# A fused transformer-style block on one core: four steps of the delta branch stand one slot later in a hand-written schedule

## The reference, cut to what matters

```python
x = x + 0.5 * ffn(layernorm(x))          # first pass through the experts
x = x + mamba(layernorm(x))              # selective scan block
x = x + 0.5 * ffn(layernorm(x))          # second pass, same weights

def mamba(x):                            # x: 32 sequences x 256 tokens x 128 channels
    x_in, z = split(x @ W_in + b_in)     # 256 inner channels each
    x_conv = silu(causal_conv4(x_in) + conv_b)
    Bm, Cm = split(x_conv @ W_xp + b_xp)             # 16 states each
    delta = softplus(x_conv @ W_dt + b_dt)           # the "step size", 256 channels
    h[t] = exp(delta * A) * h[t-1] + delta * x_conv * Bm[t]      # for each of 16 states
    y = sum over states of h * Cm + D_skip * x_conv
    out = (y * silu(z)) @ W_out + b_out
    return alpha * (x + out - mean) / (std + eps) + beta

def ffn(x):                              # 8 experts of width 176, top 2, plus a shared one of width 352
    w = softmax weights of the two largest of x @ Wg
    return sum_e w[e] * ((silu(x @ W1[e]) * (x @ W2[e])) @ W3[e]) + (silu(x @ Ws1) * (x @ Ws2)) @ Ws3
```

## Time and profile before

| what | value |
| --- | --- |
| median of the runs | 1838.47 us (1837.09 to 1841.13) |
| profiled execution, own time | 1839.04 us |
| its span, first to last instruction | 1837.3 us |
| mean granted TensorE clock | 0.959 of full |
| ACT table loads at the decays, the silus, `in0`/`in1`, `sp_ln` | 124, 111, 30, 16, of 1283 ns each |

### The profile page before, as it was taken

One profiled execution on the slowest core, in us unless ns is written; L12 is line 12 of the kernel. 1 busy time (PEld: TensorE's weight loads), 2 busy tenths in 40 slices (PEclk: granted clock), 3 DMA queues, 4 the chain that ended last, 5 costly groups with the idle time before them and its releaser, 6 DMA issues.

```text
span 1837.3 us, 24041 instructions
## 1 busy us (share of the span) xinstructions
PE 1658.7 (90%) x7378; PEld 1001.5 (55%) x7378; DVE 1478.3 (80%) x2241; ACT 1266.2 (69%) x2030; POOL 1445.7 (79%) x1366
## 2 busy tenths in 40 slices
PE   5898788999999999999999999999999999958488
PEld 3454445556555555656555555656555555534255
DVE  1438889989798988989798988989898998989732
ACT  2367678787877778776867777786877777665422
POOL 3336869888898988888888888888898888887753
PEclk9998889999999999999999999999999999969599
DMA  6026768687776868686777867777677868767642
GB/s 158 24 87 141 180 150 193 160 205 173 185 184 162 207 156 201 158 194 170 178 184 170 201 158 189 181 187 184 168 190 172 196 156 192 184 152 186 143 104 69
DMA packets 121287, 304.54 MB, mean 166 GB/s; under 512 B 19299, under 2 KB 40518, under 8 KB 106822
## 3 DMA queue, kind: packets, MB, share of 16 engines
q0 software_dynamic: 18432, 125.84, 34.4%
q1 hardware_dynamic: 98406, 174.46, 33.3%
q10 hardware_dynamic: 4320, 2.71, 0.5%
HBM read 167.67 MB, written 5.24 MB: 94 GB/s over the span
## 4 chain that ended last, share of the span: by engine, by line
POOL 43%; DMA 23%; issue 14%; PE 9%; DVE 7%; ACT 1%; SPq 1%; POOLq 0%; ACTq 0%; DVEq 0%
DMA yacc<-prod 19%; POOL prod L623 18%; POOL gated L555 14%; DVE hist L924 4%; DMA crow<-c_rows 3%; POOL yacc L619 2%; PE ps_y L1090 2%; DVE ps_db L876 2%; POOL yacc L640 1%; PE ps_h1a L1076 1%; SPq L418 1%; PE ps_h2a L1098 1%; PE ps_h1b L1076 1%; PE ps_h2b L1098 1%; POOL xres L610 1%
## 5 line engine op out<-in xcount | busy, mean ns | idle before, releaser
L623 POOL TENSOR_TENSOR prod<-hist,crow 128x1024 f32<-128x1024 f32 x224 | 556.5, 2484 | 204.7 <-DVE hist L924 171.0
L1090 PEld LDWEIGHTS ps_y<-down_w,gated 128*128 128x128 f32 (+1 forms) x3584 | 474.0, 196 | 276.4 <-issue 160.1
L924 DVE TENSOR_TENSOR_SCAN hist<-decay,ps_db 128x1024 f32<-128x1024 f32 x256 | 583.3, 2278 | 2.8
L555 POOL TENSOR_TENSOR gated<-gated,silu 128x512 f32<-128x512 f32 x352 | 493.3, 1450 | 74.4 <-DVE gated L904 71.4
L1090 PE MATMUL ps_y<-down_w,gated 128*128 128x128 f32 (+1 forms) x3584 | 491.8, 282 | 58.0 <-POOL gated L555 56.3
L876 DVE TENSOR_TENSOR ps_db<-du,ps_db 128x1024 f32<-128x1024 f32 x256 | 313.2, 1224 | 114.2 <-PE ps_db L1058 112.1
L686 ACT ACTIVATE decay<-delta,a_neg 128x510 f32<-128x510 f32 x512 | 326.8, 709 | 3.7 <-DVE delta L965 2.2
L706 ACT ACTIVATE silu<-ps_h1a 128x512 f32<-128x512 f32 (+1 forms) x224 | 132.9, 593 | 194.8 <-PE ps_h1a L1076 194.6
L1076 PE MATMUL ps_h1b<-xnT,up_w 128*128 128x512 f32 x448 | 236.7, 610 | 3.6 <-ACT silu L706 3.1
L1098 PE MATMUL ps_h2a<-xnT,up_w 128*128 128x512 f32 (+1 forms) x448 | 236.1, 609 | 1.9 <-DVE gated L904 1.9
L1076 PE MATMUL ps_h1a<-xnT,up_w 128*128 128x512 f32 (+1 forms) x448 | 236.4, 609 | 0.0
(11 more groups left out here) (136 smaller groups left out, 1937.5 us busy)
## 6 DMA issues: line engine op xcount, KB each, us to landing
yacc<-prod POOLq DMA_DIRECT2D x112, 1024.0 KB, 10.0
crow<-c_rows SPq DMA_DIRECT2D x128, 512.0 KB, 5.0
wrow<-w_rows SPq DMA_DIRECT2D x320, 128.0 KB, 6.3
wrow<-w_rows SPq DMA_DIRECT2D x64, 224.0 KB, 7.0
wrow<-w_rows SPq DMA_DIRECT2D x64, 192.0 KB, 6.4
wrow<-w_rows SPq DMA_DIRECT2D x64, 160.0 KB, 2.9
yacc<-yacc POOLq DMA_DIRECT2D x16, 512.0 KB, 7.8
wrow<-w_rows SPq DMA_DIRECT2D x64, 96.0 KB, 2.9
```

The costliest lines, as they stand in the source:

```text
L555: nc.gpsimd.tensor_tensor(gated[:, pos % NGATE, :], gated[:, pos % NGATE, :], silu[:, (pos + NCHUNK * f_parity(of, f)) % NSILU, :], ALU.mu ...
L623: nc.gpsimd.tensor_tensor(prod[:, (pair - 1 + odd) % 2, s % 2, :, :], hist[:, s % 2, :, :], c_all, ALU.mult).then_inc(prod_done, 1)
L924: nc.vector.tensor_tensor_scan(hist[:, s % 2, :, :].rearrange("p h t -> p (h t)"), decay[:, s % NA, :, :, :].rearrange("p h b t -> p (h b ...
L1090: ins = nc.tensor.matmul(ps_y[:, t * C:(t + 1) * C], gated[0:rd, posd % NGATE, t * P:(t + 1) * P], down_w[0:rd, jd, :], start=(posd == 0 a ...
```

## The change

`dt1` goes from slot 18 to slot 19, `sp_exp` and `xproj` from slot 20 to 21, `sp_ln` from slot 22 to 23. `dt0`, `bparts`, `bsplit` and `delta` stay. In slot 19 `dt1` stands ahead of `stats1`, in slot 23 `sp_ln` stands ahead of `xT1`. `sp_exp` still comes last in its slot on ACT, behind the decays, but slot 21 has none. `START_PLAN` follows `PLAN`.

The rest of the diff puts the helpers that count semaphore values in another form: the functions that could take k as a register value lose that case, and the counts (`turn`, `ffn_no`, `route_no`, `stats_no`, the norms' chain) are looked up in lists that are made from the plan once. The plans are reached through dictionaries, and each step may name another iteration than the slot's own; no entry does so. The order of all other steps and what each waits for stay the same.

```diff
-        15: ["in3", "ln_scale"], 16: ["wT0", "ln_shift"], 17: ["dt0"], 18: ["dt1", "ln_add"], 19: ["stats1"],
-        20: ["sp_exp", "xproj", "scale1"], 21: ["addy1"], 22: ["norm1", "sp_ln", "bparts"], 23: ["xT1", "bsplit"], 24: ["logits1"],
+        15: ["in3", "ln_scale"], 16: ["wT0", "ln_shift"], 17: ["dt0"], 18: ["ln_add"], 19: ["dt1", "stats1"],
+        20: ["scale1"], 21: ["addy1", "sp_exp", "xproj"], 22: ["norm1", "bparts"], 23: ["sp_ln", "xT1", "bsplit"], 24: ["logits1"],
...
+    ALL = [(name, it) for k in range(-2, G + 2) for slot in range(SLOTS) for name, it in steps(k, slot)]
+    MISC = {step: n + 1 for n, step in enumerate(s for s in ALL if s[0] in MISC_NAMES)}
...
+    def turn(it, name):
+
+        return MISC[(name, it)]
...
-                    if "sp_exp" in plan(k).get(slot, []) and lead(k):
-
-                        act.wait_ge(softplus_chain, (HALVES + 1) * (k + 2) - 1)
-                        nc.scalar.activation(dtmp[:], dtmp[:], ACT.Exp, scale=-1.0).then_inc(softplus_chain, 1)
-
-            iterations(act, body)
+                    for step, it in steps(k, slot):
+                        if step == "sp_exp":
+
+                            act.wait_ge(softplus_chain, (HALVES + 1) * (it + 2) - 1)
+                            nc.scalar.activation(dtmp[:], dtmp[:], ACT.Exp, scale=-1.0).then_inc(softplus_chain, 1)
```

More of the change, by code:

```diff
@@ L91, in macaron_kernel @@
     }
[L93 to L100, removed]
     SETUP_MADE, SETUP_TAPS, SETUP_EDGE = 16, 24, 28
-    def first(k):
-        return isinstance(k, int) and k == -2
+    PLANS = {k: START_PLAN for k in range(-2, FULL)}
+    UNITS = {k: START_UNIT for k in range(-2, FULL)}
+    SP_PLANS = {k: START_SP for k in range(-2, FULL)}
     def enters(k):
-        return not isinstance(k, int) or 0 <= k + 2 < G
+        return 0 <= k + 2 < G
@@ L126, in before @@
[L126 to L187, removed]
+        return 0 <= k - 2 < G
@@ new lines, in macaron_kernel @@
+    ROLES = [(enters, ["stats0", "scale0", "norm0", "xT0", "logits0", "rcopy0", "route0", "tilt0", "weights0", "wT0"]),
+             (lead, ["addy0", "stats2", "scale2", "norm2", "xT2", "in0a", "in0", "in1a", "in1", "in2", "in3", "dt0", "dt1",
+                     "sp_exp", "sp_ln", "xproj", "bparts", "bsplit", "cT", "bT", "delta", "du"]),
+             (tail, ["fold", "gate_y0", "gate_y1", "outproj", "resid", "stats3", "scale3", "ln_norm", "ln_scale",
+                     "ln_shift", "ln_add", "stats1", "scale1", "norm1", "xT1", "logits1", "rcopy1", "route1", "tilt1",
+                     "weights1", "wT1"]),
+             (last, ["addy1"])]
@@ L189, in iterations, with w_turn, unit, home @@
+    def w_turn(it, f, e):
+        n = ECHUNK * ffn_no(it, f) + e
+        return n % NW, 2 * 16 * (n // NW + 1)
+    def unit(k, slot, lag):
+        return UNIT_AT.get((k + 2) * SLOTS + slot - lag)
+    def home(group):
+        return group % XS
+    def iterations(body):
         for k in range(-2, G + 2):
@@ L422, in body @@
                 for slot in range(SLOTS):
[L423 to L445, removed]
@@ L707, in body @@
+                        nc.scalar.activation(silu[0:r, (pos + NCHUNK * f_parity(of, f)) % NSILU, :],
                                              ps_h1[pos % 2][0:r, :], ACT.Silu).then_inc(silu_done, 1)
-                    for step in plan(k).get(slot, []):
-                        if step == "xT0" and enters(k) or step == "xT1" and tail(k) or step == "xT2" and lead(k):
-                            take(k, step)
+                    for step, it in steps(k, slot):
+                        nxt, entering, ahead, behind = 1 - it % 2, home(it + 2), home(it + 1), home(it - 1)
+                        if step == "xT0" or step == "xT1" or step == "xT2":
+                            take(it, step)
@@ L1166, in body @@
                             ins.then_inc(misc_full, 1)
-                    if slot == SETUP_EDGE and first(k):
+                    if slot == SETUP_EDGE and k == -2:
                         make_edge()
```

448 lines of the change are left out of this document (246 added, 202 removed).

## The result

The changed kernel takes **1854.42 us** (median of 4 runs, 1853.21 to 1862.09), the kernel before beside it 1839.8 (1837.09 to 1841.81). The ratio is 1.0089 (95% interval 1.0072 to 1.0107), some 15 to 16 us. The profiled execution is the slowest of the four, 1862.09 with a span of 1860.4; the other three are 1853.21, 1853.84 and 1855.0.

What follows compares the result with a forecast made beforehand. It took PE, 96% busy, as the bound, with `row_b(24)` setting short iterations; twelve times 2.67 us (32.0) less 9.9 swallowed by long iterations gave +22.1 us: 1861.1 for the profiled execution, median 1860, range 1842 to 1872.

Steps and rivals of the forecast that it cites:

- Part 1: `dt1` to slot 19: its 1.03 us wait goes, PE waits 2.0 us for POOL instead, `row_b(20)` 0.9 us later.
- Part 2: `xproj` to slot 21: the same work stands ahead of `row_b(22)` in either order, so nothing from there on.
- Part 3: `sp_exp` to slot 21: two more table loads, transposes of `norm1`'s tile wait 1.8 us, `row_b(24)` 2.67 us later in all.
- whatever delays `row_b(24)` lengthens a short iteration one for one: From slot 24 on: a late `row_b(24)` lengthens a short iteration equally, 2.67 us each, 32.0 us over twelve iterations.
- Part 4: `sp_ln` to slot 23: no further cost; `logits1` keeps 0.22 us, `h1` of slot 27 may wait 0.4, covered in slot 29.
- The `wrow` waits: DVE's waits for router weights in slot 26: the long iterations swallow 9.9 us of the delay in all.
- The clock: Rival, chance 0.07: PE's two new waits per iteration bring the granted clock down, 12 x 0.75 us more, 1869 us.
- Edges: k = -1 to 1 and k = 14: costed at nothing, each within plus or minus 1.03 us, 4 us together.

## Why the prediction was right

Direction, size and most single steps held; the median of 1854.42 lies 6 us under the 1860 predicted. That the profiled execution (1862.09) came out within 1 us of the sum made for it (1861.1) owes something to two errors that cancel.

- **Part 1: right.** A wait for POOL stands in slot 19 (1.83 us, 2.0 in the prediction), none ahead of `dt1`; `row_b(20)` is 0.87 late (0.9). Undone on POOL's side, it goes.
- **Part 2: right for this change, not as a rule.** Nothing in slots 20 to 22 here (6.25 for 6.33), where all is 0.87 late already. The reason given, that the same work stands ahead of `row_b(22)` in either order, overlooks that the order decides whether PE waits for POOL's chunk in slot 21: 0.28 us with `xproj` alone, 0.75 where slot 19 no longer holds.
- **Part 3: right as far as `row_b(24)`.** 24 loads more; the transposes wait 1.73 (1.80); `row_b(24)` is 2.74 late (2.67). The Trainium skill (ScalarE: Activation LUTs, What ACT_TABLE_LOAD costs) has a drain of 1380 ns besides the load; the wait above was forecast with the load alone and came out 0.07 shorter, so the trace speaks against the drain here.
- **The step that failed: "whatever delays `row_b(24)` lengthens a short iteration one for one".** Of 2.74, an iteration is longer by 1.68. The step rested on DVE having "no idle time" from `row_b(24)` to the end of scan 13. DVE was busy without a break, but not all of it was work. Rows of before, DVE and POOL in slot 24:

```profile
1331.82 1.80 DVE L959 TENSOR_TENSOR hot<-lanes,topi 128x64 f32<-128x64 f32 x1
...
1333.54 1.22 DVE L876 TENSOR_TENSOR ps_db<-du,ps_db 128x1024 f32<-128x1024 f32 x1
```

```profile
1331.18 2.36 POOL L623 TENSOR_TENSOR prod<-hist,crow 128x1024 f32<-128x1024 f32 x1
```

  and after:

```profile
1139.52 0.65 DVE L955 TENSOR_TENSOR hot<-lanes,topi 128x64 f32<-128x64 f32 x1
...
1140.09 1.22 DVE L874 TENSOR_TENSOR ps_db<-du,ps_db 128x1024 f32<-128x1024 f32 x1
```

```profile
1137.73 2.35 POOL L629 TENSOR_TENSOR prod<-hist,crow 128x1024 f32<-128x1024 f32 x1 [0.76 <-DVE hist L919]
```

  The same small product of 64 columns takes 1.80 us before, 0.65 after, and 0.23 in the kernel with `sp_exp` alone. In both kernels it ends within 0.1 us of POOL's product (1333.62 and 1333.54; 1140.17 and 1140.08). That is no accident of one row: of the 32 in the changed kernel's trace, 29 start while a POOL instruction runs and end 0.07 to 0.09 us after it, and the other three take 0.22 to 0.23. So the 1.15 us that are gone from DVE's "busy" time here were waiting for POOL. And POOL's product, which started in an unbroken run before and behind a wait of 0.76 after, is only 1.6 later by `row_b(18)` (26.70 and, less the clock's 1.67, 28.29 us behind it). POOL set the pace of slots 24 to 26, and `row_b(24)` had 1.1 us to spare. That agrees with the end, 1.68. `du` in slot 28 shows the same: 1.91 us before and 1.20 after, as it starts 2.38 us late and ends 1.67 late. The Trainium skill (SBUF — State Buffer, SBUF: two separate sides) says that VectorE and GpSimd share a port pair under an exclusive lock, which a VectorE instruction takes against GpSimd's reads when both its inputs lie in SBUF, and that the later one waits; both inputs of `hot` and of `du` do, and these rows agree. The 19.5 us of busy time that DVE lost on the page are these two, 12.4 and 8.0, less the 0.9 of `delta`.

  No kernel took this cause away by itself, but the other traces bear it out. At the full clock and without a wait for `wrow`, us later or longer than before:

  | kernel (k) | `row_b(24)` | POOL's product, slot 24 | `hot` takes | iteration |
  | --- | --- | --- | --- | --- |
  | `xproj` alone (4) | 0.46 | 0.48 | 1.81 | 0.49 |
  | changed, `sp_exp` in 20 (4) | 0.77 | 0.78 | 1.79 | 0.77 |
  | `dt1` alone (5) | 0.88 | 0.89 | 1.81 | 0.90 |
  | changed, `ln_shift` in 17 (11) | 1.52 | 0.60 | 0.87 | 0.55 |
  | changed (10) | 2.74 | 1.59 | 0.64 | 1.69 |

  The iteration follows POOL's product and not `row_b(24)`. In two kernels it follows neither, as PE waits for ACT besides: `sp_exp` alone (1.79, 0.64, longer by 2.06) and `norm1` in slot 21 (0.77, 0.76, longer by 1.65).
- **Part 4: right in its size, 0, for another reason than given.** `logits1` does not wait at all, where the prediction kept its 0.22 us. `h1` of slot 27 waits 0.65 (0.4). Slot 29's wait for POOL, named as its cover, is indeed used up, and `du`'s hidden wait of 0.7 with it.
- **The `wrow` waits: right.** The long iterations swallow their part: 14.4 us of waits become 2.1.
- **The clock: named as a rival, mis-sized, and true in part.** It was given 0.75 us in all twelve iterations. It took about 1.68 us in five (k = 3, 5, 7, 9, 11 of the profile).
- **Edges: costed at nothing, 3.8 us here.** Up to k = 1 it is 1.5 (k = 1 alone takes 97.46 for 95.01), from k = 14 on 2.3. The sum is within the 4 stated; k = 1 by itself, 2.45, is beyond the 1.03 given to each. The 1.5 is not clear of chance: the kernel with the entries of before reaches `row_b(18)` of k = 2 at 367.74 us, the kernel before at 366.41.

**The balance of the profiled executions.** Eleven iterations of 104.94 in place of 103.2 make 19.1, and the twelfth (k = 13, 103.77 for 102.09) 1.7, together 20.8. The 10.9 of long iterations before are gone, and 9.4 of long iterations after stand in their place, of which the clock's are 5 x 1.68 = 8.4. That is +19.3, and 3.8 at the edges makes 23.1, the difference of the spans (1860.4 - 1837.3). In the prediction it was 32.0 - 9.9 = 22.1: 11 us too much for the one-for-one step, and some 12 too little for clock and edges. In the three other executions, 7 to 9 us shorter, fewer clock falls would account for the difference (four or five of them). Their mean granted clocks, 0.964, 0.961 and 0.962 beside 0.960, go that way, but they have no trace that shows it.

## What to carry to other kernels

Before moving a step past a wait, ask which engine is late next, and look at the engine whose product the following instruction takes: here a wait of 1.03 us was exchanged for one of 1.83. A busy engine isn't an engine at work: compare one instruction's duration at its several places, because a row that is longer than its like can hide a wait, and with it slack, as `hot` did (1.80 us against 0.22). And when an iteration comes in two lengths, look first at the DMA queue: one load issued ahead of a store that waits for its own completion was worth more here (0.8%) than any order of the compute steps tried.

## What the runs showed that was not expected

A wait of 1.83 us of PE brought a fall of the granted clock in some iterations and not in others, with nothing different in the program: 5 of 12 in the changed kernel's profile, 4 with `dt1` alone, 5 with `sp_exp` back, 5 with `norm1` in slot 21. Each cost about 1.7 us, nearly as much as the wait. With 0.61 us at the same place the clock fell there in none of the twelve iterations of any of the four profiles that have it, nor before the change, where PE waited 1.03 us ahead of `dt1`. With `sp_exp` alone it fell in 4 of 12 behind the wait of 1.28 us for the copy. So the spread of a kernel's runs (1841.3 to 1856.8 with `sp_exp` back) can be part of what a change does.
